# Five of the sixteen value-weight products moved into the first two units of latent attention

## The reference

```python
x = x + cross_attention(layernorm(x), ctx_2048, mask)          # stage x
x = x + latent_attention(layernorm(x), ...)                    # stage m
x = x + ffn(layernorm(x), ...)                                 # stage f

def latent_attention(x, ...):                                  # 16 heads
    q = rmsnorm(x @ wq_a.T + b) @ wq_b.T + b                   # latent 384, then heads of 128 + 64
    kv, k_pe = split(x @ wkv_a.T + b)                          # 128 and 64
    q_pe, k_pe = rope(q_pe), rope(k_pe)
    q_nope = einsum('bshd,hdc->bshc', q_nope, wkv_b[:, :NOPE]) # into the latent space
    scores = (q_nope . kv + q_pe . k_pe) / sqrt(192), causal, softmax
    out = einsum('bsht,btc->bshc', scores, kv)
    out = einsum('bshc,hdc->bshd', out, wkv_b[:, NOPE:])
    return out.reshape(...) @ wo.T + b
```

## Time and profile before

| | before |
|---|---|
| median of 3 runs | 1141.07 us |
| profiled execution | 1138.37 us |
| its span | 1136.6 us |
| TensorE matmul busy | 1095.0 us, 96% |
| TensorE weight loads busy | 950.7 us, 84% |
| VectorE busy | 532.7 us, 47% |
| ScalarE busy | 352.5 us, 31% |
| GpSimd busy | 322.0 us, 28% |
| mean granted TensorE clock | 0.991 |

### The profile page before, as it was taken

One profiled execution on the slowest core, in us unless ns is written; L12 is line 12 of the kernel. 1 busy time (PEld: TensorE's weight loads), 2 busy tenths in 40 slices (PEclk: granted clock), 3 DMA queues, 4 the chain that ended last, 5 costly groups with the idle time before them and its releaser, 6 DMA issues.

```text
span 1136.6 us, 20925 instructions
## 1 busy us (share of the span) xinstructions
PE 1095.0 (96%) x8097; PEld 950.7 (84%) x8097; DVE 532.7 (47%) x998; ACT 352.5 (31%) x699; POOL 322.0 (28%) x370
## 2 busy tenths in 40 slices
PE   4799999899999999999999999999999999999996
PEld 2567676888888889888888888979899998989895
DVE  1566567444344444443444446755253343526242
ACT  1465655222222222222222224523131222213130
POOL 1243353121211212111211221435152433425151
PEclk9899999999999999999999999999999999999998
DMA  9999931101111020201111016501010110101000
GB/s 360 361 411 419 412 140 51 52 11 43 57 42 53 22 68 18 59 29 41 55 42 55 28 57 195 204 1 38 1 37 1 38 37 1 37 0 38 1 19 19
DMA packets 41913, 100.96 MB, mean 89 GB/s; under 512 B 7883, under 2 KB 12382, under 8 KB 37374
## 3 DMA queue, kind: packets, MB, share of 16 engines
q1 hardware_dynamic: 41854, 100.16, 24.7%
HBM read 74.45 MB, written 17.30 MB: 81 GB/s over the span
## 4 chain that ended last, share of the span: by engine, by line
PE 90%; DVE 3%; issue 2%; DMA 2%; SPq 2%; ACT 1%; POOL 1%; DVEq 0%; POOLq 0%; ACTq 0%
PE b_z L44 6%; PE b_z L46 6%; PE b_z L45 6%; PE b_score L44 5%; PE b_prob L44 5%; PE b_prob L46 5%; PE b_score L46 5%; PE b_score L45 5%; PE b_prob L45 5%; PE b_z L1082 3%; PE b_read L44 2%; PE b_free L44 2%; PE b_read L46 2%; PE b_read L45 2%; PE b_free L46 2%; PE b_free L45 2%
## 5 line engine op out<-in xcount | busy, mean ns | idle before, releaser
L813 POOL TENSOR_TENSOR m_e<-m_e,m_rs 128x512 f32<-128x512 f32 x32 | 34.7, 1084 | 358.2 <-DVE m_rs L960 358.2
L1416 POOL TENSOR_TENSOR f_hT_lo<-f_h,f_hT_hi 128x512 fp32r<-128x512 f32 x64 | 89.4, 1397 | 94.5 <-ACT f_hT_hi L1459 89.7
L44 PE MATMUL b_z<-m_zT_lo,m_wq_hi 128*128 128x256 f32 x384 | 108.7, 283 | 0.0
L45 PE MATMUL b_z<-m_zT_hi,m_wq_lo 128*128 128x256 f32 x384 | 108.7, 283 | 0.0
L46 PE MATMUL b_z<-m_zT_hi,m_wq_hi 128*128 128x256 f32 x384 | 108.7, 283 | 0.0
L1515 DVE TENSOR_TENSOR f_h<-f_h 128x512 f32<-128x512 f32 x64 | 70.6, 1104 | 61.4 <-ACT f_h L1454 61.4
L901 DVE TENSOR_TENSOR m_pT_lo<-b_turn,m_pT_hi 128x512 fp32r<-128x512 f32 x32 | 22.1, 692 | 160.4 <-ACT m_pT_hi L860 160.4
L854 ACT ACTIVATE m_qT<-b_z,m_q_bias 128x256 f32<-128x256 f32 x128 | 53.7, 471 | 79.2 <-PE b_z L46 75.4
L44 PEld LDWEIGHTS b_z<-m_zT_lo,m_wq_hi 128*128 128x128 f32 x384 | 73.7, 192 | 0.0
L45 PEld LDWEIGHTS b_z<-m_zT_hi,m_wq_lo 128*128 128x128 f32 x384 | 73.7, 192 | 0.0
L46 PEld LDWEIGHTS b_z<-m_zT_hi,m_wq_hi 128*128 128x128 f32 x384 | 73.7, 192 | 0.0
(11 more groups left out here) (222 smaller groups left out, 3161.6 us busy)
## 6 DMA issues: line engine op xcount, KB each, us to landing
x_ctx_in<-ctx_rows_dram SPq DMA_DIRECT2D x16, 1024.0 KB, 9.8
x_ctxT<-ctx_turned_dram SPq DMA_DIRECT2D x15, 1024.0 KB, 9.7
m_swapped<-m_by_sin SPq DMA_DIRECT2D x128, 64.0 KB, 2.0
z_scratch<-x_zbuf SPq DMA_DIRECT2D x16, 288.0 KB, 8.8
m_raw<-attn_raw_dram SPq DMA_DIRECT2D x6, 768.0 KB, 11.2
m_z_in<-z_scratch SPq DMA_DIRECT2D x8, 576.0 KB, 3.7
x_x_all<-x_dram SPq DMA_DIRECT2D x16, 256.0 KB, 9.8
x_scratch<-x_x_all SPq DMA_DIRECT2D x16, 256.0 KB, 9.4
```

Of the source, the lines that this page charges most:

```text
L44: nc.tensor.matmul(out, lh, rl, start=first, stop=False)
L45: nc.tensor.matmul(out, ll, rh, start=False, stop=False)
L813: q.tensor_tensor(e[:], e[:], rs[:].unsqueeze(2).broadcast_to([P, HB, SEQ]), ALU.mult).then_inc(s["normed"], 1)
L1416: g.tensor_tensor(hT_lo[:, 2 * n:2 * n + 2].rearrange("p m n -> p (m n)"), h[:, n % 2], hT_hi[:, 2 * n:2 * n + 2].bitcast(F32).rearrange(" ...
```

## The change

Five value products (`LATE = 5`) are taken out of the stretch ahead of the units. The stretch is now 8 products, the latents' turns, 3 products, the keys' turn. The other five stand inside units 0 and 1: three in unit 0 between the query products and the scores, two in unit 1 between the turn of the probabilities and the weighing. They don't use the ring: their banks are score, prob, read, score, prob, which the output projection and the keys use otherwise. ScalarE casts and VectorE subtracts them in the same units, in unit 0 behind `q_part` and `rotate`, in unit 1 behind `probs`. The wait for all low parts moves from ahead of the units to unit 2, ahead of the first projection; ahead of the units TensorE waits for the 23 early ones. The counts of all instructions stay the same.

```diff
--- before.py
+++ after.py
@@ -871,14 +871,21 @@
                 act.wait_ge(s["p_turned"], u)
...
 
-            def slot(g, n, u):
+            def slot(g, n, u, values_hi):
+                head = isinstance(u, int)
                 if runs(g, n, 1):
...
                         q_part(n, u, h)
+                if head and u == 0:
+                    for j in range(3):
+                        values_hi(HEADS - w.LATE + j)
                 if runs(g, n, 1):
                     probs(u - 1)
+                if head and u == 1:
+                    for j in range(3, w.LATE):
+                        values_hi(HEADS - w.LATE + j)
                 if n == 3 and has_next(g):
...
                         latent(g + 1, j)
@@ -891,7 +898,8 @@
                     if n == 3 and has_next(g):
...
 
-            return dict(latent=latent, keys=keys, groups=lambda: slots(act, slot), exp=exp, q_part=q_part,
+            return dict(latent=latent, keys=keys, exp=exp,
+                        groups=lambda values_hi: slots(act, lambda g, n, u: slot(g, n, u, values_hi)), q_part=q_part,
                         probs=probs, out=out)
         def vector(dve):
@@ -965,15 +973,22 @@
                     dve.wait_ge(s["x1_biased"], T2 * (g + 1))
...
 
-            def slot(g, n, u):
+            def slot(g, n, u, values_lo):
+                head = isinstance(u, int)
                 if runs(g, n, 1):
...
                     rotate(n, u)
+                if head and u == 0:
+                    for j in range(3):
+                        values_lo(HEADS - w.LATE + j)
                 if runs(g, n, 1):
...
                     probs(u - 1)
+                if head and u == 1:
+                    for j in range(3, w.LATE):
+                        values_lo(HEADS - w.LATE + j)
                 if n == 3 and has_next(g):
...
                         latent(g + 1, j)
@@ -987,10 +1002,10 @@
                         values(g)
...
 
-            def groups():
+            def groups(values_lo):
                 dve.wait_ge(s["tables"], 48)
                 dve.wait_ge(s["consts"], 2)
-                slots(dve, slot)
+                slots(dve, lambda g, n, u: slot(g, n, u, values_lo))
 
...
                         mask=mask, shift=shift, residual=residual)
@@ -1102,17 +1117,28 @@
                                             stop=j == T2 - 1)
...
 
-            def slot(g, n, u):
+            def slot(g, n, u, fill_values):
                 def before(lag):
...
 
+                head = isinstance(u, int)
                 if runs(g, n):
                     q_unit(g, n, u)
+                if head and u == 0:
+                    for j in range(3):
+                        if j == 2:
+                            pe.wait_ge(s["k_done"], 1)
+                        fill_values(HEADS - w.LATE + j)
+                if head and u == 2:
+                    pe.wait_ge(w.s["lo"], w.FILLS)
                 if runs(g, n, 2):
...
                     turn_probs(u - 1)
+                if head and u == 1:
+                    for j in range(3, w.LATE):
+                        fill_values(HEADS - w.LATE + j)
                 if n == 3 and has_next(g):
...
                 if runs(g, n, 2):
@@ -1130,8 +1156,8 @@
                     turn_scores(u)
...
 
-            def groups():
-                slots(pe, slot)
+            def groups(fill_values):
+                slots(pe, lambda g, n, u: slot(g, n, u, fill_values))
 
...
                         project=project, turn_probs=turn_probs, weigh=weigh, scores=scores,
@@ -1152,6 +1178,7 @@
     ROPE_ROUNDS = 2
...
     RAW_LOADS = 1 + QUERY_LOADS
+    LATE = 5
 
...
         self.nc, self.A, self.mem, self.banks = nc, A, mem, banks
@@ -1162,6 +1189,9 @@
                   "vec_loaded raw_loaded last_loaded turned cols filled hi lo biased q_bias rope".split()}
     def bank(self, f):
+        late = f - (self.FILLS - self.LATE)
+        if late >= 0:
+            return (self.banks.score, self.banks.prob, self.banks.read, self.banks.score, self.banks.prob)[late]
         return self.banks.ring[f % self.R]
     def key_cols(self, f):
@@ -1236,7 +1266,8 @@
         def fill_values(j):
...
             pe.wait_ge(s["last_loaded"], 48)
-            pe.wait_ge(s["lo"], f - (self.R - 1))
+            late = f - (self.FILLS - self.LATE)
+            pe.wait_ge(s["lo"], f - (self.R - 1) if late < 0 else f - late if late < 3 else f - 2)
             t.matmul(self.bank(f)[:], mem.values_raw[:, j], mem.out_raw[:, j], start=True, stop=True).then_inc(s["filled"], 1)
         return dict(fill_keys=fill_keys, fill_bias=fill_bias, fill_values=fill_values)
@@ -1725,16 +1756,16 @@
             x["scale_q"](L, L % 2)
...
                 w["keys_hi"](f)
-            for j in range(12):
+            for j in range(8):
                 w["values_hi"](j)
...
             m["latent"](0, 1)
-            for j in range(12, HEADS):
+            for j in range(8, HEADS - weights.LATE):
                 w["values_hi"](j)
...
             act.wait_ge(weights.s["q_bias"], 1)
-            m["groups"]()
+            m["groups"](w["values_hi"])
             f = F["scalar"](act)
...
             for h in range(4):
@@ -1792,14 +1823,14 @@
             for f in range(9, weights.KEY_FILLS):
...
             w["bias"]()
-            for j in range(12):
+            for j in range(8):
                 w["values_lo"](j)
...
             m["latent"](0, 1)
-            for j in range(12, HEADS):
+            for j in range(8, HEADS - weights.LATE):
                 w["values_lo"](j)
             dve.wait_ge(weights.s["q_bias"], 1)
-            m["groups"]()
+            m["groups"](w["values_lo"])
             f = F["vector"](dve)
...
             f["first_var"](0, 0)
@@ -1857,20 +1888,20 @@
             for f in range(5, weights.KEY_FILLS):
...
             w["fill_bias"](X)
-            for j in range(12):
+            for j in range(8):
                 w["fill_values"](j)
...
             m["turn_latent"](0, 1)
-            for j in range(12, HEADS):
+            for j in range(8, HEADS - weights.LATE):
                 w["fill_values"](j)
...
             pe.wait_ge(weights.s["rope"], 3 * weights.ROPE_ROUNDS)
-            pe.wait_ge(weights.s["lo"], weights.FILLS)
+            pe.wait_ge(weights.s["lo"], weights.FILLS - weights.LATE)
             pe.wait_ge(weights.s["q_bias"], 1)
-            m["groups"]()
+            m["groups"](w["fill_values"])
             f = F["tensor"](pe)
...
             m["project"](G, 1, U - 2, 0)
```

## The result

The changed kernel takes 1134.69 us, median of 8 runs (1134.07 to 1136.12), against 1140.10 for the kernel before, median of 8 (1138.12 to 1145.45): 5.41 us less, ratio 0.9951 with a 95% interval of 0.9938 to 0.9965. In a later comparison (e10) the ratio was 0.9960, 0.9944 to 0.9976; one run of the kernel before in it took 6061 us, counts as slow and is left out of the ratio. The forecast was 5.6 us. The first interval stands for 4.0 to 7.1 us: the change is clear of no change, but the time alone would also fit the 4.2 and 4.8 us of the first two rivals, and the stage times have to decide between them.

The account below looks back on a forecast made before the run. TensorE, carrying 90% of the chain of waits, was taken as the bound. 4.30 + 1.52 - 0.10 - 0.10 = 5.6 us faster: 1132.8 from the profiled execution, 1135.5 against the median; range 1131.5 to 1140.0 us.

Parts of the forecast that it names:

- the first two rivals: Clock falls in any case, 4.2 us gained, chance 0.12; VectorE's queue late in unit 0, 4.8 us gained, chance 0.08.
- The five products, 4.30: Ahead of the units: five value products at 0.86 us removed, so everything from the key turn on starts 4.30 us earlier.
- The waits priced at nothing: Latent turns coming 3.44 us earlier: their load and stored-latents waits cost nothing, at most 3.44 us lost.
- the products stick out: Unit 0: three products outlast the gap before the scores by 0.06 us, taken as 0.10, bounds 0 and 0.35.
- The tie that I could not resolve: Unit 0's masks just in time for the score turn, by 0.14 us; taken at nothing, range 0 to 0.8.
- The two products: Unit 1, ahead of the weighing: two products cost nothing, at worst 0.1 us.
- The clock, 1.52: Unit 0's scores to unit 1's first query product: filling the gap avoids the low clock, gaining 1.52 us, bounds 0 and 1.52.
- The first rival: The clock falls in any case, perhaps elsewhere: only 4.2 us gained, 1136.9 us; chance 0.12.
- VectorE was not late: Rival in unit 0: kv_lo keeps 1.35 or a split is held, masks 0.8 us late, 4.8 gained; chance 0.08.
- The gap was idle: Rival: TensorE was held by something not shown, so the five products cost 4.30 us again; 1139.6 us, chance 0.04.
- The low clock did not multiply: Rival in units 0 to 3: repeated falls cost 1.5 us each, four give 1143.0 us; chance 0.03.
- the class slower: Outcome class for the whole kernel, beside faster 0.50 and within 0.5% 0.46; given 0.04.

Follow-up runs that it names:

- e10: The changed kernel unchanged, a third look: ratio 0.9960 of the kernel before, median 1135.87 us.
- e3: The kernel before with three extra value products, results unread, added in the gap of unit 0: ratio 0.9992 of the kernel before.
- e5: The kernel before, unchanged, profiled once more: 36.63 us from the first value product to the weighing.
- e12: The changed kernel with a sixth product moved, three in each of units 0 and 1: 30.64 us to the weighing, single time 1130.68 us.
- e1: The kernel before with only the three products of unit 0 moved, none into unit 1: ratio 0.9986 of the kernel before.
- e2: The kernel before with only two products moved, into unit 1, gap of unit 0 left open: ratio 0.9985 of the kernel before.
- e4: The kernel before with one product moved into unit 0 and two into unit 1: ratio 0.9974 of the kernel before.
- e7: The changed kernel with the split of the values (kv_hi, kv_lo) ahead of unit 0's three new casts and splits: single run 1136.61 us.
- e9: The kernel before, unchanged, a third look: 36.62 us from the first value product to the weighing.
- e8: The changed kernel with the one-column bias products put two behind each of the first eight value products: ratio 0.9954 of the kernel before.
- e11: The changed kernel with bias products spread between the first eight value products, timed again: ratio 0.9956 of the kernel before, median 1135.38 us.

## Why the prediction was right, and what it left out

**The five products, 4.30.** The keys' turn comes at 10.18 instead of 14.48, 4.30 earlier. Its wait was met: the second latent split ended at 190.52 + 0.55 = 191.07, 0.79 ahead (predicted 0.8). The waits priced at nothing cost nothing either: the latents' turns began at 188.63, 0.86 behind the start of the product before them.

**Unit 0.** The prediction put the scores at 204.21 on the clock of before, which is 19.71 in this measure; they came at 19.77. So the products stick out by 0.16, not 0.10 (0.15 in e3, 25.76 against e5's 25.61). kv_lo took 0.42 and the masks ended at 22.28 (predicted 22.36), ahead of the score turn at 22.56 (22.50). The tie that I could not resolve did not cost anything.

**The stage behind it.** 4.30 instead of 5.83, with full clock. First query product of unit 1 at 24.07 (24.02), turn of the probabilities 28.39 (28.34), weighing 30.78 (30.73).

**Unit 1.** The two products are hidden entirely: the weighing stands 2.39 behind the turn, as before. e12 shows that the room is used up.

**The clock, 1.52.** The price was right and the reason was not. The prediction said "The low clock follows this gap and no other", reasoned from the gap's length (2.37 with a fall, 1.79 without), and took the fall for a property of every execution. Its own trace had a longer gap that it did not count, in stage f, with the clock full behind it (a row of the timeline, then two windows of the kernel before):

```profile
742.68 0.47 PE L44 MATMUL b_score<-f_down_lo,f_hT_hi 128*128 128x512 f32 x1 [2.68 <-issue]
740.00:745.00 5.00, 2.32 (x10) 1.99 (x11) 5.00 (x3) 3.05 (x2) 5.00 (x2) 1.00 0.01 3
745.00:750.00 5.00, 5.00 (x23) 4.13 (x22) 4.40 (x5) 0.77 (x3) 4.17 (x2) 1.00 0.00 0
```

All fourteen profiled executions have that gap. The clock was low behind it in seven (after, e1, e2, e4, e7, e9, e10) and full in the other seven; the kernel before is on both sides (low in e9, full in the first execution and in e5). From the weighing to the end the seven took 920.4 to 921.3 us, the others 918.8 to 920.0. So neither the length of a gap nor the kernel decides alone.

In the changed stage it is the same. Three executions of the kernel before show the gap of unit 0 with a low clock behind it once, and twice with none: there the low stretch, and its cost, came some 20 us earlier, behind the bias products. All three had exactly one, and the two places cost nearly the same, which is why their stage times agree within 0.2 (36.45 to 36.63). In the changed kernel the gap is closed, but the place behind the bias products is still open: two of its executions are at 30.8, one at 32.5. So the change gives 5.8 us (36.6 - 30.8) in an execution of it without a low stretch and 4.1 (36.6 - 32.5) in one with it. Of all twelve executions with the bias products in one stretch, five have it there. With 5 in 12 the mean would be 5.8 - 0.42 x 1.7 = 5.1 us, an estimate from these few executions; the measured ratios, 0.9951 and 0.9960 (5.6 and 4.6 us), lie about it. The same reckoning gives e3 1.5 x 7/12 - 0.1 = 0.8 us (measured 0.9) and e2 its 1.7 (1.7), both within wide intervals, but not e1's 1.6. That the measured time came as near to 5.6 as it did is in part luck.

The first rival, that the clock falls in any case, was given 0.12. It is what one execution in three of the changed kernel shows, only not at a place that I had looked at: the profile of before had no low clock there.

**The other rivals.** VectorE was not late: kv_lo took 0.42 behind the addition, and no split was held up beside it. That the rival's case would have cost time was not run. In e7 kv_lo takes 1.35 ahead of the splits, where VectorE had been idle for 3.63, and costs nothing; in its place behind them, 0.93 more would by these rows have put the masks 0.65 behind TensorE's turn, an estimate (they ended 0.28 ahead of it). The gap was idle (e3). The low clock did not multiply in units 0 to 3. In the chances, the class slower was given 0.04 and its only rival 0.03; a hundredth of it has no source.

## What to carry to other kernels

Work for TensorE that no one waits for yet can be put into the gaps of a pipeline's first units, as long as its banks are free there and its readers' queues have room; count the gap from the releaser's end, and it fills to within 0.2 us. A term for the clock read from one execution is a term with a probability. First see whether every like gap of the same trace has the low clock behind it, then profile the same kernel several times before you give the term its full weight. Compare kernels of this size by the length of the changed stage: its start alone scatters by 3.7 us here.

## What the runs showed of the hardware

Past the start and ahead of the end of the kernel, the clock was found at the lower level (0.50, 1.2 GHz) behind two kinds of stretches, and never behind either in every execution. One is a gap in which TensorE did nothing: 2.4 us in unit 0 (low in 2 of 4 executions that have it: before and e2, not e5 and e9) and 2.7 us in stage f (7 of 14). The other is one of 3.5 us of continuous one-column matmuls in which both TensorE rows count it as fully busy (5 of 12). Where it had been low behind the second, it was not low again behind the gap of unit 0 some 20 us later (e5, e9), and with neither gap nor one-column stretch this stage was at full clock in both executions (e8, e11). A low stretch cost 1.5 us behind the gap of unit 0 and 1.7 us among the value products. What decides in which execution it comes is not shown.

The runs also settle a price that stood as a range: kv_lo, with two operands in SBUF, takes 1.35 us beside GpSimd's addition and 0.42 without it. By the Trainium skill (SBUF — State Buffer, "Who interferes with whom") such an instruction of VectorE and one of GpSimd that reads SBUF contend, and the later of the two is blocked until the other is through. The trace agrees: kv_lo ended 0.28 us after the addition in the kernel before and in e7, while a value split, with one operand in PSUM, could stand beside the addition at 0.69 (200.46, in the changed kernel):

```profile
200.46 0.69 DVE L1306 TENSOR_TENSOR m_wvo_lo<-b_score,m_wvo_hi 128x512 fp32r<-128x512 f32 x1 [3.94 <-ACT m_wvo_hi L1286]
```
